# Relations' products tile by tile in the layernorm, and the basis matrices mixed beside row scatters

## The reference

```python
x = x + _L2_ffn_ref(_layernorm(x, axis=-1)[None], ...)[0]   # 32 small experts, one for each node
x = x + _L3_gnn_ref(_layernorm(x, axis=-1), basis, w_comp, bias, src, dst, etype)
# in _L3_gnn_ref:
wr = basis.reshape(in_dim, NUM_BASES, out_dim)
weight = jnp.einsum('rb,ibo->iro', w_comp, wr).reshape(num_rels, in_dim, out_dim)
t = jnp.einsum('nd,rdo->rno', h, weight)          # 8 relations x 3125 nodes x 256
msg = t[etype, src]
agg = jax.ops.segment_sum(msg, dst, num_segments=h.shape[0])
return jax.nn.relu(agg + bias)
```

## Time and profile before

| what | us |
|---|---|
| median of three runs | 5994.16 |
| the profiled execution, its span | 5993.39, 5991.4 |
| row scatters of the small experts | 37.0 |
| layernorm with the picks | 40.0 |
| mixing | 29.6 |
| products | 176.2 |
| mean granted clock of PE over the span | 0.92 |

### The profile page before, as it was taken

One profiled execution on the slowest core, in us unless ns is written; L12 is line 12 of the kernel. 1 busy time (PEld: TensorE's weight loads), 2 busy tenths in 40 slices (PEclk: granted clock), 3 DMA queues, 4 the chain that ended last, 5 costly groups with the idle time before them and its releaser, 6 DMA issues. The chain is left out here.

```text
span 5991.4 us, 76018 instructions
## 1 busy us (share of the span) xinstructions
PE 4811.8 (80%) x20908; PEld 3028.3 (51%) x20909; DVE 3234.3 (54%) x7653; ACT 1665.3 (28%) x4129; POOL 3190.8 (53%) x3457
## 2 busy tenths in 40 slices
PE   7968887888778688879967994999987668888674
PEld 2233334333445333348847993888854433433364
DVE  8964444444365677769972115666656332444432
ACT  4930002000132588842223331333322111000121
POOL 3237773777435477746625764776710212777324
PEclk7979998999988899989988996999998779999887
DMA  5023333333311466665526762333310534333265
GB/s 210 11 61 105 102 104 70 105 104 104 72 40 33 125 203 201 199 170 157 155 78 213 219 188 87 116 116 114 114 35 1 149 99 130 103 104 103 54 186 170
DMA packets 392039, 705.47 MB, mean 118 GB/s; under 512 B 117903, under 2 KB 257231, under 8 KB 391567
## 3 DMA queue, kind: packets, MB, share of 16 engines
q0 software_dynamic: 131680, 338.79, 20.9%
q1 hardware_dynamic: 256800, 359.35, 19.0%
q10 hardware_dynamic: 3216, 3.28, 0.2%
HBM read 529.09 MB, written 172.09 MB: 117 GB/s over the span
## 5 line engine op out<-in xcount | busy, mean ns | idle before, releaser
L789 PE MATMUL ps<-wide 128*128 128x256 f32 x2640 | 917.8, 430 | 317.1 <-DMA wide<-table,src 189.1
L816 DVE TENSOR_TENSOR wide<-wide,ps 128x256 f32 x1320 | 555.0, 420 | 979.1 <-PE ps L789 976.6
L774 POOL DMA_INDIRECT wide<-table,src x880 | 850.8, 967 | 276.6 <-PE ps L789 203.3
L789 PEld LDWEIGHTS ps<-wide 128*128 128x128 f32 x2640 | 408.0, 190 | 839.8 <-DMA wide<-table,src 554.1
L786 PE MATMUL ps<-zerow,zerob 128*128 128x440 bf16 x2640 | 714.7, 353 | 27.9 <-DVE wide L127 27.9
L774 POOL DMA_INDIRECT wide<-table_rel,rel x440 | 427.7, 972 | 351.5 <-ACTq L96 217.7
L2488 POOL DMA_INDIRECT work<-table,work x440 | 451.6, 1026 | 187.7 <-issue 105.9
L1658 POOL DMA_INDIRECT wide<-table_gat,src x440 | 452.8, 1029 | 134.2 <-issue 134.2
L1677 PE MATMUL ps<-wide,work 128*128 128x512 f32 x880 | 455.8, 600 | 0.0
L1638 ACT ACTIVATE wide<-ident,wide 128x128 f32<-128x128 f32 x1320 | 416.5, 388 | 81.7 <-DMA wide<-table_gat,src 78.6
L786 PEld LDWEIGHTS ps<-zerow,zerob 128*128 128x128 bf16 x2640 | 260.3, 99 | 223.8 <-DVE wide L127 29.5
(11 more groups left out here) (488 smaller groups left out, 8993.9 us busy)
## 6 DMA issues: line engine op xcount, KB each, us to landing
edge_rows<-wide SPq DMA_DIRECT2D x110, 520.0 KB, 3.0
wide<-edge_rows SPq DMA_DIRECT2D x110, 520.0 KB
normed<-in_L_ffn_W SPq DMA_DIRECT2D x42, 1024.0 KB
table_rel<-wide SPq DMA_DIRECT2D x25, 1024.0 KB, 4.4
wide<-in_L_ffn_expert_w SPq DMA_DIRECT2D x90, 256.0 KB, 3.0
work<-rec SPq DMA_DIRECT2D x110, 136.0 KB, 2.4
rec<-work SPq DMA_DIRECT2D x27, 544.0 KB, 16.3
normed_T<-in_L_ffn_W SPq DMA_DIRECT2D x14, 1024.0 KB
```

The lines of the kernel that those rows point to most:

```text
L774: nc.gpsimd.indirect_dma_start(rows[:, w % RT, :], None, table, bass.IndirectOffsetOnAxis(ap=index[:, w:w + 1], axis=0)).then_inc(gathered ...
L789: nc.tensor.matmul(m.PS[:, w % (2 * Q), 0:D], S[:, w % RT, :], rows[:, w % RT, :], start=True, stop=True).then_inc(summed, 1)
L816: v.tensor_tensor(at, at, m.PS[:, s, 0:D], ALU.add).then_inc(added, 1)
```

## The change

`layernorm` takes an object `product` and calls it at fixed places in the orders of SP, DVE, ACT and PE. `ByRelation` is that object: it holds the products' matmuls, copies and stores. PE makes the products of tile n-2 after the transposes of tile n; ACT copies the first half of tile n-3's products after it has evicted tile n; DVE copies the second halves in runs between `normal` and `moments`. The transposes keep banks 0 to 3, the products have 4 to 7. The products read `m.XT` itself, so ACT's staging ring is gone. `send_and_mix` takes the place of `send_rows` for the small experts: SP loads w_comp and basis ahead of the experts' weights, POOL builds the mask ahead of its scatters, and DVE and PE mix as the old stage did (not shown), into `m.AF`. The old stages 4 and 5 are taken out. Other calls of `layernorm` stay as they were.

```diff
@@ -589,11 +589,13 @@
-def layernorm(nc, m, src, dst, dstT, picks=0, shared=True, ready=None):
+def layernorm(nc, m, src, dst, dstT, picks=0, shared=True, ready=None, product=None):
 
     GROUPS = NT // U
     BY_ACT = 2
-    LAST_BY_DVE = 2
+    LAST_BY_DVE = 0 if product else 2
+    RT = 4 if product else 8
+    LAG, BEHIND = 2, 3
     with Stage(nc) as st:
         names = ("dstep", "half", "whole", "vared", "rooted", "shifted", "normed_v", "normed_a", "turned", "evicted")
         (dstep, half, whole, vared, rooted, shifted, normed_v, normed_a, turned, evicted) = (st.sem(s) for s in names)
...
-        block = st.block()
+        if product:
+            product.prepare(st, evicted)
+        block = st.block()
+        if product:
+            @block.sync
+            def _(sp):
+                product.loads(sp)
+                product.stores(sp)
...
                     normal(g)
+                if product:
+                    for n in range(max(g * U - BEHIND - U + 1, 0), g * U - BEHIND + 1):
+                        product.by_dve(dve, n, order[n])
                 if g + 1 < GROUPS:
                     moments(g + 1)
                 if not picks:
                     normal(g)
+            if product:
+                for n in range((GROUPS - 1) * U - BEHIND + 1, NT):
+                    product.by_dve(dve, n, order[n])
...
             def evict(n):
                 t = order[n]
                 act.wait_ge(turned, n + 1)
-                nc.scalar.copy(dstT[:, :, t * P:(t + 1) * P], m.PS[:, n % 8, 0:D].rearrange("p (k n) -> p k n", k=KD)
+                nc.scalar.copy(dstT[:, :, t * P:(t + 1) * P], m.PS[:, n % RT, 0:D].rearrange("p (k n) -> p k n", k=KD)
                                ).then_inc(evicted, 1)
+                if product and n >= BEHIND:
+                    product.by_act(act, n - BEHIND, order[n - BEHIND])
...
+            if product:
+                for n in range(NT - BEHIND, NT):
+                    product.by_act(act, n, order[n])
...
-                if n >= 8:
-                    pe.wait_ge(evicted, n - 7)
+                if n >= RT:
+                    pe.wait_ge(evicted, n - RT + 1)
...
+                if product and n >= LAG:
+                    product.multiply(pe, n - LAG, order[n - LAG])
+            if product:
+                for n in range(NT - LAG, NT):
+                    product.multiply(pe, n, order[n])
...
+def send_and_mix(nc, m, a, beside):
+
+    NR, NB, IL = 8, 4, 16
+    w = view(m.AF, 0, KD * NR * D).rearrange("p (k r d) -> p k r d", k=KD, r=NR)
+    mixer = m.AF[0:IL * NB, KD * NR * D:KD * NR * D + P]
+    comp = m.AF[0:IL * NB, KD * NR * D + P:KD * NR * D + P + NR]
+    spare = m.XT[:].rearrange("p k n -> p (k n)")
+    basis = spare[0:IL * NB, 0:NR * KD * D].rearrange("p (q d) -> p q d", d=D)
+    with Stage(nc) as st:
+        sent, came, loaded, masked, mixed, made, taken = (
+            st.sem(s) for s in ("sent", "came", "loaded", "masked", "mixed", "made", "taken"))
+        block = st.block()
+
+        @block.sync
+        def _(sp):
+            for i in range(IL):
+                sp.dma_start(comp[i * NB:(i + 1) * NB, :], a["L3_gnn_w_comp"]).then_inc(loaded, 16)
+            sp.dma_start(basis, a["L3_gnn_basis"].rearrange("b i d -> (b i) d").rearrange("(q p) d -> p q d", p=IL * NB)
+                         ).then_inc(loaded, 16)
+            sp.wait_ge(came, 16 * beside(sp, came))
+
+        @block.gpsimd
+        def _(pool):
...
+            for t in range(NT):
+                g.indirect_dma_start(m.rows_in, bass.IndirectOffsetOnAxis(ap=m.forth[:, 0, t:t + 1], axis=0),
+                                     m.XN[:, t, :], None).then_inc(sent, 16)
+            pool.wait_ge(sent, 16 * NT)
+
...
-    send_rows(nc, m, 1, weights_in)
+    send_and_mix(nc, m, a, weights_in)
...
+class ByRelation:
+
+    NR = 8
+
+    def __init__(self, nc, m):
+        self.nc, self.m = nc, m
+        self.w = view(m.AF, 0, KD * self.NR * D).rearrange("p (k r d) -> p k r d", k=KD, r=self.NR)
+        self.outs = [view(m.BB, s * self.NR * D, self.NR * D) for s in range(U)]
+
+    def prepare(self, st, evicted):
+        self.evicted = evicted
+        self.made, self.taken_a, self.taken_v = (st.sem(s) for s in ("w_made", "taken_a", "taken_v"))
+        self.stored = st.sems("stored", U)
+
...
+    def stores(self, sp):
+        to = self.m.table_rel.rearrange("(r t p) d -> p t r d", p=P, t=NT)
+        for n in range(NT):
+            g, s = divmod(n, U)
+            t = g * U + (s + 2) % U
+            sp.wait_ge(self.taken_a, 2 * n + 2)
+            sp.wait_ge(self.taken_v, 2 * n + 2)
+            sp.dma_start(to[:, t, :, :], self.outs[n % U].rearrange("p (r d) -> p r d", r=self.NR)
+                         ).then_inc(self.stored[n % U], 16)
+        for s in range(U):
+            sp.wait_ge(self.stored[s], 16 * (NT // U))
+
...
+    def multiply(self, pe, n, t):
+        pe.wait_ge(self.evicted, n + 1)
+        for q in range(4):
+            if n and q % 2 == 0:
+                pe.wait_ge((self.taken_a, self.taken_v)[q // 2], 2 * n)
+            for k in range(KD):
+                mm = self.nc.tensor.matmul(self.m.PS[:, 4 + q, :], self.m.XT[:, k, t * P:(t + 1) * P],
+                                           self.w[:, k, 2 * q:2 * q + 2, :].rearrange("p r d -> p (r d)"),
+                                           start=(k == 0), stop=(k == KD - 1))
+            mm.then_inc(self.made, 1)
+
+    def by_act(self, act, n, t):
+        if n >= U:
+            act.wait_ge(self.stored[n % U], n // U * 16)
+        for q in range(2):
+            act.wait_ge(self.made, 4 * n + q + 1)
+            self.nc.scalar.copy(self.outs[n % U][:, q * 512:(q + 1) * 512], self.m.PS[:, 4 + q, :]
+                                ).then_inc(self.taken_a, 1)
+
+    def by_dve(self, dve, n, t):
+        if n >= U:
+            dve.wait_ge(self.stored[n % U], n // U * 16)
+        for q in range(2, 4):
+            dve.wait_ge(self.made, 4 * n + q + 1)
+            self.nc.vector.tensor_copy(self.outs[n % U][:, q * 512:(q + 1) * 512], self.m.PS[:, 4 + q, :]
+                                       ).then_inc(self.taken_v, 1)
+
+
 def relations(nc, m, a):
-    layernorm(nc, m, m.X, m.XN, m.XT, picks=1, shared=False)
...
+    layernorm(nc, m, m.X, m.XN, m.XT, picks=1, shared=False, product=ByRelation(nc, m))
```

More of the change, by code:

```diff
@@ L613, in _ @@
                                                  ).then_inc(came[t], 16)
+            if product:
+                product.aside(pool)
         @block.vector
@@ L2080, in _ @@
             pool.wait_ge(sent, 16 * picks * NT)
+def send_and_mix(nc, m, a, beside):
[18 more added lines that the diff above has]
+        def _(pool):
+            g = nc.gpsimd
+            mv = mixer.rearrange("p (i r) -> p i r", r=NR)
+            g.memset(mixer, 1.0).then_inc(masked, 1)
+            pool.wait_ge(masked, 1)
+            g.affine_select(out=mv, in_=mv, compare_op=ALU.is_ge, fill=0.0, base=0, pattern=[[-NB, IL], [0, NR]],
+                            channel_multiplier=1).then_inc(masked, 1)
+            pool.wait_ge(masked, 2)
+            g.affine_select(out=mv, in_=mv, compare_op=ALU.is_ge, fill=0.0, base=NB - 1,
+                            pattern=[[NB, IL], [0, NR]], channel_multiplier=-1).then_inc(masked, 1)
+            for t in range(NT):
+                g.indirect_dma_start(m.rows_in, bass.IndirectOffsetOnAxis(ap=m.forth[:, 0, t:t + 1], axis=0),
+                                     m.XN[:, t, :], None).then_inc(sent, 16)
+            pool.wait_ge(sent, 16 * NT)
+        @block.vector
+        def _(dve):
+            dve.wait_ge(masked, 3)
+            dve.wait_ge(loaded, 16 * (IL + 1))
+            mv = mixer.rearrange("p (i r) -> p i r", r=NR)
+            nc.vector.tensor_tensor(mv, mv, comp.unsqueeze(1).to_broadcast([IL * NB, IL, NR]), ALU.mult
+                                    ).then_inc(mixed, 1)
+            for q in range(NR * KD):
+                dve.wait_ge(made, q + 1)
+                nc.vector.tensor_copy(w[:, q % KD, q // KD, :], m.PS[:, q % 4, 0:D]).then_inc(taken, 1)
+        @block.tensor
+        def _(pe):
+            pe.wait_ge(mixed, 1)
+            for q in range(NR * KD):
+                if q >= 4:
+                    pe.wait_ge(taken, q - 3)
+                nc.tensor.matmul(m.PS[:, q % 4, 0:D], mixer, basis[:, q, :], start=True, stop=True).then_inc(made, 1)
@@ L2861, in _ @@
             pipeline(dve, R, (2, shape), (0, finish), total=W)
-def relations(nc, m, a):
-    NR, NB = 8, 4
-    layernorm(nc, m, m.X, m.XN, m.XT, picks=1, shared=False)
[L2867 to L2875, removed]
-        block = st.block()
[L2878 to L2980, removed]
-                        nc.vector.tensor_copy(outs[s][:, q * 512:(q + 1) * 512], m.PS[:, q, :]).then_inc(taken_v, 1)
@@ new lines, with loads, aside, begin @@
+class ByRelation:
[8 more added lines that the diff above has]
+        self.stored = st.sems("stored", U)
```

(10 more changed lines are left out.)

7 lines of the change are left out of this document (5 added, 2 removed).

## The result

The changed kernel takes 6013.35 us (median of eight executions, from 6004.57 us up; one of them took 14237.09 us at a mean granted clock of 0.356, where the others had 0.92, and has no part in the ratio), the kernel before, run beside it, 5994.29 (5986.2 to 5999.86). The ratio is 1.0028, interval 1.0019 to 1.0038: 0.28% slower, 19 us by the medians. The profiled execution took 6015.7 us.

A forecast was written before the change was run, and what follows sets the result against it. PE was taken to bound the products. The rebuilt stage's terms summed to 260.9 us against 245.7, 15.2 more; with 2.5 in the send stage, 17.7 on 5993.39 gave 6011 us, 80% range 5997 to 6032.

The forecast's parts named there:

- first product after the first gather: Start of the rebuilt stage: PE's first product matmul starts 16.4 us after the first gather, once ACT has evicted tile 0.
- 25 tiles of products: PE in the rebuilt stage: 25 tiles of product matmuls at full rate, 6.87 us each, take 171.8 us.
- first product at half rate: PE at the start of the products: it begins at half rate, as in the kernel before, costing 2.6 us.
- 19 short waits: PE before a tile's products: idles 1.63 us for ACT's copies queued behind an eviction, 19 times, 31.0 us.
- 3 long waits: PE at M(3), M(8), M(13): idles 6.85 us each as ACT's root, awaiting DVE's moments, precedes the copies; 20.6 us.
- restarts: PE after each wait: weight load not hidden, 0.11 us for 22 restarts, plus half of 2.4 for transposes; 3.6 us.
- clock behind long waits: PE after the three long waits: granted clock falls to 0.50, costing 2.0 us each, 6.0 us in all.
- clock behind short waits: PE after the 19 short waits: clock falls with chance 5/52, costing 1.8 us each; 3.2 us, bounds 0 and 34.
- The rival of a clock that falls at every tile: Rival, products: the clock falls after every short wait, costing 34 us in place of 3.2; 6042 us, chance 0.10.
- The clock holds: Rival, products: waits as computed, but no clock fall behind any wait and no restart cost; 5998 us, chance 0.17.
- PE doesn't wait: Rival, products: ACT reaches tile n-3's copies before tile n's transposes end, so PE never waits; 5947 us, faster case 0.13.
- The send stage: Small experts' row scatters: added POOL instructions and SP loads lengthen it by 2.5 us, bounds 1.1 and 5; mixing hidden.

The follow-up runs named there:

- e1: Changed kernel, but ACT copies tile n-3's products ahead of its wait for tile n's transposes and that tile's eviction; 5978.86 us, 0.9974 times the kernel before.
- e2: Changed kernel, with only the copies of tile 5g-3 moved ahead of ACT's wait for the next group's moments (three places); 5984.44 us, 0.9981 times the kernel before.
- e11: The changed kernel itself run once more, with no further edit; 6020.2 us beside 6000.39 of the kernel before, ratio 1.0032.
- e12: Changed kernel with 60 matmuls of zeros on PE in each of its three long waits; 6009.79 us, 1.0016 times the kernel before.
- e5: Changed kernel with ACT's copies of tile n-3 ahead of every eviction and ahead of the root at the group's edge; 5951.85 us, 0.9928 times the kernel before.
- e8: e5 plus first three tiles evicted before the second group's root, 40 matmuls of zeros at stage start, one w_comp load for sixteen; 5940.89 us, ratio 0.991.

## Why the prediction was right

6013.35 against 6011, for the reason given; the terms of the sum, from the trace after:

| term | predicted | measured |
|---|---|---|
| first product after the first gather | 16.4 | 16.39 |
| 25 tiles of products | 171.8 | 172.0 (25 x 6.88, e1) |
| 22 transposes | 4.8 | 4.6 (0.21) |
| first product at half rate | 2.6 | 3.1 |
| last copy | 0.9 | 0.9 |
| 19 short waits | 31.0 | 32.3 (1.70) |
| 3 long waits | 20.6 | 20.8 (6.92) |
| restarts | 3.6 | 1.4 |
| clock behind long waits | 6.0 | 6.8 |
| clock behind short waits | 3.2 | 0 |
| sum | 260.9 | 258.3 |

In the terms of the prediction, the waits are taken from the start of T(n) to the start of M(n-2), 1.91 and 7.13, less the 0.21 that this takes in a stream; the profile's 1.53 and 6.75 count from the modelled end of T(n), drain and all. The chain of steps behind each wait (result, semaphore, eviction, copies, semaphore) held to 0.07 us, and so did the longer one through DVE's moments. The steps as listed add up to 1.80 and 7.04, so 1.58 and 6.82 without T(n)'s 0.22, where the prediction took 1.63 and 6.85; against the steps themselves the measured 1.70 and 6.92 are 0.12 and 0.10 longer.

*Sizes that were off.* Restarts (the longer first matmul after a wait): an M after a wait ends 7.11 us after its start, not 7.03, and a T pays nothing; the 0.11 from the 256-column pair was too much for this shape, and half of it for the transposes was a guess that fell. The clock behind the short waits: none of 19 lost it, nor did any of e2's, e11's or e12's; at a chance of 5 in 52, nineteen would all stay clear about one time in seven, so one kernel alone decides little, but the three others make the chance of such waits, identical and in a regular stream, smaller than that of the stages it was taken from. The long waits lost 2.7, 2.2 and 1.9 (9.61, 9.13 and 8.89 from start to next transposes, less 6.94). For these the prediction named 16 waits of 4.8 us and more out of full rate. The trace before has 32 of them, each followed by 0.50, which bears the rule out; half rate lasted 2.9 to 64 us behind them, so the 2.9 to 5 behind its 2.0 us held for a part of them only.

*The rival of a clock that falls at every tile* (6042) fell with them: the granted clock over a tile with its 1.53 us of idleness is 1.00. The Trainium skill, "TensorE: Matmul & The Clock Gate", section "A second HAM failure mode: psum-queue depth-cycling", tells of a bf16 kernel in which cycling through PSUM banks, with short idle times between groups of matmuls, made the clock swing; this trace, in float32, with four banks and a gap in every tile, doesn't show it. The stretch 2100 to 2550 that the prediction set against the page is weaker than it looks: its 1.00 is rounded, and one of the five falls lies in it, at 2202.50, behind 2.13 us of idleness. *The clock holds* (5998) fell by the long waits: e12 is that case for them, and it gives 7.1 us back. *PE doesn't wait* (5947) is no account of the change, but it is what e5 built: 5951.85.

*The send stage* grew by 3.4, inside the bounds and by the path that was forecast: the weights land late, and the last scatter lands late in their company. Of the sum's 2.5 us, 1.1 stood for POOL's start and 1.4 for the company; POOL's last scatter was issued 0.6 later in the stage, and the company cost 2.7 (5.13 less 2.40). e8 takes 2.8 us away with fifteen issues fewer (5.33 us for sixteen loads, 0.62 for one), while the 1 MB of basis stays. So it is mostly the queue of tiny issues ahead of the weights that costs, not the bytes. The mixing ended at 4690.12, with 8.5 us to spare before the weights had landed.

The stores, DVE's share and the gathers cost nothing, as costed: e5 leaves them all in place and meets 195.56. The mechanism was right, the closeness of the number in part luck. Within the fused stage, 2.8 us by which waits, half rate and the rest came out larger stood against 5.4 us of restarts and clock that did not come; the touched stages gave +16.1 where 17.7 was forecast, and 2.9 us that no term stands for made up for it. The untouched stages of two profiles can differ by some 5 us, so a miss of 2 us says little of how exact the sum was.

## What to carry to other kernels

When work of two engines is laced together by hand, follow each instruction that frees a buffer back through its own queue: a copy that could run at once costs a wait in every turn if an instruction that waits for the engine it feeds stands ahead of it. Here, exchanging a few lines moved the stage from 258 to 196 us, between 0.3% slower and 0.7% faster than before, with the same instructions. Count a long wait of TensorE with what the clock takes behind it (here 6.9 and 2.3 us), and don't take the same price for short ones in a steady rhythm.

## What was not expected of the hardware

- Nineteen equal waits of 1.53 us, every 8.85 us, left the granted clock at 1.00 each time, where elsewhere in the trace before 5 of 52 such gaps were followed by a fall. What sets these apart is open.
- Matmuls of zeros in a wait held the full rate through 6.7 us in which nothing useful ran, and those at the stage's start saved 2.5 us of it (191.59 to 189.13).
- The mixing's 32 matmul records of 64 rows keep PE busy for 14.02 us on end and the granted clock stays at 0.50 in that stretch, before and after.
- A load that comes late lengthens another queue's transfer beside it: the last scatter landed 2.40 us after its issue with the weights already there, and 5.13 with their last bytes beside it.
- One chip ran the kernel before in 6681.79 us, the others in 5994 to 6000, with a mean granted clock of 0.84 where they had 0.92. Its long waits (6.75) were the same to 0.01 us.
